# Expert outputs stored in tile order, fetched by slot in the attention that follows

## The reference

```python
# second experts: 4096 rows, two of 8 experts for each, at most 256 rows for each expert
top_vals, top_ids = top_k(x_flat @ router_w.T + router_b, 2)
top_probs = softmax(top_vals)
for e in range(8):
    tok, slot = nonzero(top_ids == e, size=256, fill_value=(N, 0))   # the first 256 rows
    y = (xin @ W[e]) * silu(xin @ V[e]) @ W_out[e]                   # xin = rows tok
    out[tok] += y * top_probs[tok, slot]
# third attention: keys and values from the normed context and from normed x (the latents),
# queries from the latents, 16 heads of 64
```

## Time and profile before

| | |
|---|---|
| time, median of three runs | 1677.85 us (1676.03 to 1679.96) |
| time of the profiled execution | 1677.99 us |
| its span, first to last instruction | 1676.1 us |
| TensorE matmul busy | 1402.1 us (84%) |
| VectorE busy | 1116.0 us (67%) |
| ScalarE busy | 894.4 us (53%) |
| GpSimd busy | 766.5 us (46%) |
| mean granted TensorE clock, share of full | 0.896 |
| queue of GpSimd's DMAs | 12448 packets, 26.21 MB |

### The profile page before, as it was taken

One profiled execution on the slowest core, in us unless ns is written; L12 is line 12 of the kernel. 1 busy time (PEld: TensorE's weight loads), 2 busy tenths in 40 slices (PEclk: granted clock), 3 DMA queues, 4 the chain that ended last, 5 costly groups with the idle time before them and its releaser, 6 DMA issues. The chain is left out here.

```text
span 1676.1 us, 37474 instructions
## 1 busy us (share of the span) xinstructions
PE 1402.1 (84%) x10866; PEld 1300.1 (78%) x10867; DVE 1116.0 (67%) x3509; ACT 894.4 (53%) x2715; POOL 766.5 (46%) x766
## 2 busy tenths in 40 slices
PE   6687699956867389999999999999998499567398
PEld 4566599945646289999999999999997499444298
DVE  5646744458777457777777777877776466686455
ACT  4454155532223168777878787778775133244254
POOL 3066345420003445555657575757454356303344
PEclk9797799977667789999999999999999699878599
DMA  9312112240131400000000000000000333521322
GB/s 223 41 33 60 49 56 63 63 157 24 51 110 41 127 13 2 14 1 19 9 15 11 1 24 0 25 0 13 1 14 9 105 82 85 191 66 52 114 78 71
DMA packets 88412, 88.54 MB, mean 53 GB/s; under 512 B 17058, under 2 KB 74761, under 8 KB 87927
## 3 DMA queue, kind: packets, MB, share of 16 engines
q1 hardware_dynamic: 72472, 58.10, 12.6%
q0 software_dynamic: 12448, 26.21, 4.8%
q10 hardware_dynamic: 3392, 3.02, 0.7%
HBM read 53.98 MB, written 34.82 MB: 53 GB/s over the span
## 5 line engine op out<-in xcount | busy, mean ns | idle before, releaser
L2101 POOL TENSOR_TENSOR paired_rows<-paired_rows,rinv 128x1024 f32<-128x1024 f32 x128 | 242.5, 1894 | 243.6 <-DVE rinv L2416 227.2
L2407 DVE TENSOR_TENSOR probs_turned_lo<-psum_banks,probs_turned_hi 128x512 fp32r<-128x512 f32 x256 | 175.9, 687 | 141.1 <-ACT probs_turned_hi L2266 137.5
L2292 ACT ACTIVATE paired_rows<-psum_banks,neg_max 128x256 f32<-128x256 f32 x512 | 236.7, 484 | 0.6 <-DVEq L1993 0.4
L2213 PE MATMUL psum_banks<-probs_turned_hi,y_rows 128*128 128x256 f32 x1024 | 213.9, 292 | 0.9 <-DVEq L1993 0.9
L2163 PE MATMUL psum_banks<-y_turned_parts,queries_hi 128*128 128x256 f32 x1024 | 199.7, 293 | 3.0 <-DVEq L1993 3.0
L2213 PEld LDWEIGHTS psum_banks<-probs_turned_hi,y_rows 128*128 128x128 f32 x1024 | 167.2, 190 | 1.7 <-DVEq L1993 1.5
L2266 ACT CAST probs_turned_hi<-psum_banks 128x512 fp32r<-128x512 f32 x256 | 151.2, 591 | 19.6 <-PE psum_banks L2134 9.6
L2163 PEld LDWEIGHTS psum_banks<-y_turned_parts,queries_hi 128*128 128x128 f32 x1024 | 158.1, 191 | 3.6 <-issue 3.6
L2134 PE MATMUL psum_banks<-ident,paired_rows 128*128 128x128 f32 x1024 | 155.6, 274 | 5.2 <-DVE probs_turned_lo L2407 2.9
L2422 DVE TENSOR_REDUCE neg_max<-psum_banks 128x4 f32<-128x1024 f32 x128 | 155.5, 1215 | 5.0 <-PE psum_banks L2163 4.7
L2163 PE MATMUL psum_banks<-y_turned_parts,queries_lo 128*128 128x256 f32 x512 | 144.8, 283 | 0.0
(11 more groups left out here) (718 smaller groups left out, 3734.0 us busy)
## 6 DMA issues: line engine op xcount, KB each, us to landing
paired_rows<-expert_rows SPq DMA_DIRECT2D x16, 512.0 KB, 6.0
expert_w_a<-rows_by_expert_last SPq DMA_DIRECT2D x39, 129.0 KB
tile_rows<-rows_by_expert_first SPq DMA_DIRECT2D x71, 64.5 KB
tile_rows<-rows_by_expert SPq DMA_DIRECT2D x71, 64.5 KB
expert_w_b<-in_L_ffn_w_dram SPq DMA_DIRECT2D x2, 2048.0 KB, 12.8
tile_rows<-expert_rows SPq DMA_DIRECT2D x8, 512.0 KB, 3.8
x_rows<-in_x_dram SPq DMA_DIRECT2D x8, 256.0 KB, 5.5
ctx_turned_dram<-ctx_turned SPq DMA_DIRECT2D x1, 2048.0 KB, 10.4
```

The lines of the kernel that those rows point to most:

```text
L2101: ins = pool.tensor_tensor(probs[:, k, :, :], probs[:, k, :, :], rinv[:, k, :].unsqueeze(2).to_broadcast([P, 4, 256]), ALU.mult)
L2213: ins = pe.matmul(bank[Z_BANK][:, r * 256:(r + 1) * 256], yrows[:, 2 * s1 + y, (2 * r + k) * P:(2 * r + k + 1) * P], probsT[x][:, (u + 1) ...
L2292: ins = act.activation(probs[:, par, h, :], bank[S_BANKS[par] + h // 2][:, (h % 2) * 256:(h % 2 + 1) * 256], ACT.Exp, bias=nmax[:, par, h: ...
L2407: ins = dve.tensor_tensor(lo, bank[bank_][:, :], hi.bitcast(F32), ALU.subtract)
```

## The change

The second experts no longer write to `ys` by pair. SyncE stores each output tile with a plain DMA of 64 KB at the tile's own place, so `ys` holds rows by slot; GpSimd only gathers. The routing keeps each pair's slot in `POS` (0 for dropped pairs, whose weight is zero) with four further columns of zeros, and no longer makes `DEST`: half of the one-hot matmuls and the VectorE operations behind them go. In the third attention a group's pairs are fetched by eight indirect gathers on GpSimd by these slots: two groups ahead of the loop, then each group in steps 13, 14 and 15 two cycles ahead of its use. Ahead of each eight, the slots of the group are copied to a small tile, GpSimd waits for that copy's semaphore, and does a tiny addition. Nine groups are fetched; the ninth, with the zero columns, is read by nobody.

```diff
-        POS = sb("slots", [P, 2, B], U32)
+        POS = sb("slots", [P, 2, B + G], U32)
@@ routing, VectorE
                     if capacity:
                         ch.link(dve.tensor_tensor(posf[:, :, :], posf[:, :, :], keep[:, :, :], ALU.mult))
+                        dve.memset(POS[:, :, B:B + G], 0)
+                        dve.tensor_copy(POS[:, :, 0:B], posf[:, :, :])
...
                     dve.tensor_scalar(SOURCE[:, 0:n_tiles], found, float(HALF), None, ALU.add)
-                    if layer in SCATTERED:
-                        ch.link(dve.tensor_copy(pair_used[:, :], first))
...
-                        dve.tensor_tensor(DEST[:, 0:n_tiles], pair_found[:, :], pair_spare[:, :], ALU.add)
@@ routing, TensorE, for each of eight pairs
-                            if layer in SCATTERED:
-                                k = r % top
-                                own = bank[7][:, (1 + k) * n_tiles:(2 + k) * n_tiles]
-                                ins = pe.matmul(own, hot_row[:, s, :, r], hot_tile[:, s, :, r], start=False, stop=True, skip_group_check=True)
@@ experts
-            expert_out = tile_scattered
+            scatters = not fixed
+            expert_out = tile_scattered if layer in KEPT else tile_loaded
@@ experts, SyncE
+                    if not scatters:
+                        for j in range(n_tiles):
+                            sp.wait_ge(expert_kept.sem, j + (expert_kept.value + 1))
+                            sp.dma_start(tile_of(ys, j), yo[:, j % SLOTS, :]).then_inc(expert_out[j % SLOTS].sem, 16)
+                        for s in range(SLOTS):
+                            sp.wait_ge(expert_out[s].sem, expert_out[s].value + 16 * in_slot(s))
@@ experts, GpSimd
-                        if i >= 0:
+                        if scatters and i >= 0:
@@ third attention, SyncE
-                    stage(0)
-                    stage(1)
                     load_expert_weights(sp, 2)
...
-                    stage(2)
-                    for n in range(3, NG):
-                        stage(n)
@@ third attention, GpSimd
+                    def gather_pairs(n, which):
+                        for x in which:
+                            j, k = x // 2, x % 2
+                            pool.indirect_dma_start(staged[:, j, k, :], None, ys[0:TILES_CAP * P, :], bass.IndirectOffsetOnAxis(ap=group_slots[:, x:x + 1], axis=0)).then_inc(pairs_staged.sem, 16)
+
+                    def slots_of(n):
+                        pool.tensor_copy(group_slots[:, :].rearrange("p (j k) -> p k j", k=2), POS[:, :, bass.ds(n * G, G)]).then_inc(slots_copied.sem, 1)
...
+                    GATHER = {13: (0, 1, 2), 14: (3, 4, 5), 15: (6, 7)}
...
+                    def begin_pairs(n):
+                        slots_of(n)
+                        pool.wait_ge(slots_copied.sem, n + 1)
+                        pool.tensor_tensor(slots_ready[:, 0:1], slots_ready[:, 1:2], slots_ready[:, 1:2], ALU.add)
@@ step
+                        if next_pairs_there(i) and c in GATHER:
+                            if c == 13:
+                                begin_pairs(i + 2)
+                            gather_pairs(i + 2, GATHER[c])
@@ ahead of the loop
+                    pool.memset(slots_ready[:, :], 0.0)
+                    begin_pairs(0)
+                    gather_pairs(0, range(2 * G))
                     norm_context(0)
+                    pool.wait_ge(pairs_combined.sem, 1)
+                    begin_pairs(1)
+                    gather_pairs(1, range(2 * G))
                     pool.wait_ge(turned_kept.sem, 1)
                     copy(0, 0, 0)
                     pool.wait_ge(turned_kept.sem, 2)
                     copy(0, 0, 1)
                     all_steps(step)(pool)
```

More of the change, by code:

```diff
@@ L278, in build @@
         leads_made = counter("leads_made")
+        slots_copied = counter("slots_copied")
         leads_exp = counter("leads_exp")
@@ L1331, in _ @@
                     dve.wait_ge(pe_done.sem, pv + 2 + (MADE if layer == 1 else 0))
-                    found, first, second = (bank[7][:, n * n_tiles:(n + 1) * n_tiles] for n in range(3))
+                    found = bank[7][:, 0:n_tiles]
                     dve.tensor_scalar(SOURCE[:, 0:n_tiles], found, float(HALF), None, ALU.add)
-                    if layer in SCATTERED:
-                        ch.link(dve.tensor_copy(pair_used[:, :], first))
[L1336 to L1343, removed]
-                        dve.tensor_tensor(DEST[:, 0:n_tiles], pair_found[:, :], pair_spare[:, :], ALU.add)
                 @block.scalar
@@ L1516, in _ @@
                                 continue
-                            to = xr[:, i % SLOTS, P:P + 1].bitcast(U32) if kept else DEST[:, i:i + 1]
+                            to = xr[:, i % SLOTS, P:P + 1].bitcast(U32)
                             pool.indirect_dma_start(ys, bass.IndirectOffsetOnAxis(ap=to, axis=0), yo[:, i % SLOTS, :], None).then_inc(expert_out[i % SLOTS].sem, 16)
-                    for s in range(SLOTS):
-                        pool.wait_ge(expert_out[s].sem, expert_out[s].value + 16 * in_slot(s))
+                    if scatters:
+                        for s in range(SLOTS):
+                            pool.wait_ge(expert_out[s].sem, expert_out[s].value + 16 * in_slot(s))
                 @block.tensor
@@ L1906, in attention_2 @@
                 group_scale = sb_in(ph, "group_scale", [P, 5, G])
+                group_slots = sb_in(ph, "group_slots", [P, 2 * G], U32)
+                slots_ready = sb_in(ph, "slots_ready", [P, 2])
                 weighted = carve(flat(Y1[:, :, :]), 16 * P, [P, G, P])
@@ L1935, in _ @@
                 def _(sp):
-                    pair_rows = ys[0:2 * B * P, :].rearrange("(t p k) d -> p t k d", p=P, k=2)
-                    def stage(n):
-                        if n:
-                            sp.wait_ge(pairs_combined.sem, n)
-                        sp.dma_start(staged[:, :, :, :], pair_rows[:, n * G:(n + 1) * G]).then_inc(pairs_staged.sem, 16)
-                    stage(0)
-                    stage(1)
                     load_expert_weights(sp, 2)
                     sp.dma_start(flat(Y1[:, 0:16, :]).rearrange("p (c d) -> p c d", d=P), A["L2_ffn_down_w"].rearrange("e (c p) d -> p (e c) d", p=P)).then_inc(weights_a.sem, 16)
-                    stage(2)
-                    for n in range(3, NG):
-                        stage(n)
                     place_pads(sp, range(E // 2))
@@ L1952, in _ @@
                     sp.wait_ge(rows_spread.sem, 16 * 2 * G * NG)
+                    sp.wait_ge(pairs_staged.sem, 16 * 2 * G * (NG + 1))
                     load_first_tiles(sp, 2)
@@ L2091, in spread, with next_pairs_there @@
                             pool.indirect_dma_start(xb, bass.IndirectOffsetOnAxis(ap=spots_of(n)[:, k, j:j + 1], axis=0), rows_of(n)[k][:, j, :], None).then_inc(rows_spread.sem, 16)
+                    GATHER = {13: (0, 1, 2), 14: (3, 4, 5), 15: (6, 7)}
+                    def next_pairs_there(i):
+                        return not isinstance(i, int) or 0 <= i < NG - 1
+                    def begin_pairs(n):
+                        slots_of(n)
+                        pool.wait_ge(slots_copied.sem, n + 1)
+                        pool.tensor_tensor(slots_ready[:, 0:1], slots_ready[:, 1:2], slots_ready[:, 1:2], ALU.add)
                     SPREAD = {3: (0, 1, 2), 6: (3, 4), 7: (5, 6), 8: (7,)}
@@ L2474, in _ @@
                     ch.link(dve.tensor_copy(ends, region))
-                    dve.wait_ge(pairs_staged.sem, 16)
+                    dve.wait_ge(pairs_staged.sem, 16 * 2 * G)
                     for k in range(2):
```

6 lines of the change are left out of this document (1 added, 5 removed).

## The result

The changed kernel takes 1684.49 us (median; 1677.71 to 1690.87) where the kernel before took 1677.68 in the same measurement (1672.88 to 1683.51). The ratio is 1.004, 95% interval 1.0027 to 1.0052, that is 6.7 us slower (4.5 to 8.7). The profiled execution took 1684.99 us, its span is 1683.1.

The account below looks back on a forecast made before the run. TensorE, 99% busy, was taken to bound the third attention's loop, but not the second experts or that attention's start. 1677.99 - 8.4 (routing and experts) + 17.1 (start) + 0 (loop) = 1686.7 us; own range 1682 to 1691, stated range 1678.0 to 1696.0.

Parts of the forecast that it names:

- Routing: End of the second routing: destinations and some TensorE waits go, a memset and copy come; 1.85 us earlier (1.4 to 2.3).
- the 0.45 for TensorE's waits: Routing: VectorE's three waits for TensorE shrink with halved matmuls; 0 to 0.9 us, taken as 0.45.
- Experts: Second experts: without scatters no tile waits for gathers; block ends 8.4 us earlier (7.0 to 8.9), routing's 1.85 included.
- the time of the last seven tiles: Second experts: after the eighth output, one more tile at 1.91 us and seven at 1.60 bring the last to 556.65.
- Start: Start of the third attention: GpSimd's gathers delay the first queries from 20.26 to 37.35 us after T0; 17.1 us lost.
- Pause: GpSimd's standstill at the third attention's start, read as a drain settling indirect DMAs; stays at 9.25 us, adding to gathers.
- Loop: Third attention's loop: 56 gathers fit beside TensorE; 0 us lost (0 to 0.5 a cycle, 3.5 in all).
- the pause was not hidden: Rival at the third attention's start: pause hidden or gone, drain costs 0.93 us, net +1.2, 1679.2 us; chance 0.20.
- did not come twice: Rival at the third attention's start: pause behind each eight gathers, 8.3 us more, 1695.0 us; chance 0.08.
- the loop's gathers kept to 1.032 us at most: Rival in the loop: stretched gathers at pitch 1.68, TensorE waits 14 us in all, 1700.7 us; chance 0.07.
- the experts did what they should: Rival in the second experts: the bound is something else, 4 us less gained, 1690.7 us; chance 0.03.
- The fourth: Rival at the third attention's start: pause shrinks, copies' drain free, queries within 25 us of T0, 1670.5 us; chance 0.07.

Follow-up runs that it names:

- the weights behind the pairs: Changed kernel plus a drain behind the experts' last gather, group 1 gathered behind the copies, weights' load issued after group 0's pairs landed: 1672.46 us, ratio 0.9959.
- plain loads: Changed kernel's routing and second experts with the third attention of the kernel before, no gathers there (adds other rows, same work): 1665.05 us, ratio 0.9901.
- the version between steps: Changed kernel plus drain behind the experts' last gather, group 1 gathered between the loop's first steps, weights after group 0's pairs: 1669.71 us; again 1669.62.

## Why the prediction was right, point by point

The forecast was +8.7 us against the profiled execution, the bold stages give +7.3 and the measurement +6.7. One sum of the prediction doesn't come out: the ends that it names for its own range (gain 7.0 to 8.9, loop up to 3.5, 2 us either way) give 1684.2 to 1693.6, and not 1682 to 1691. The result lies in both.

- **Routing**: 1.85 forecast, 1.7 found. The destinations' 1.66 went; the 0.45 for TensorE's waits was too much, as only one of the three gaps went.
- **Experts**: 6.55 forecast, 7.6 found. The step that was mis-sized is the time of the last seven tiles, which I took at 1.60 us each from a tile right behind a wait: 11.2 us. They took 10.0: one still 1.90, four 1.45, then 1.55 and 0.75. The store's landing was right (2.2 taken, 2.11 found, from the nearest rows of 2.1 and 3.8).
- **Start**: 17.1 forecast, 16.6 found. Preparation and eight gathers: 10.75 forecast, 10.5 found (564.97). Pause: kept whole at 9.25, found 8.92. Second eight gathers until 33.2, found 32.2 (586.64). The copies: their drain 1.55 us instead of 0.9. One more detail was wrong and cost nothing: the pairs landed at T0 + 13.96 and not by 12.5, with the weights' 3 MB, which SyncE now issues at 554.4 to 555.8, in flight beside them and the DMA engines 90% busy until then (the run with the weights behind the pairs has T0 + 12.07 and 18%); it stayed under the pause. As soon as the pause was short, GpSimd waited 1.03 us for VectorE.
- **The pause's cause**: right that it is the drain behind indirect DMAs and that 8 new ones neither hide nor double it. "Not linear in their number" holds as well. With all landed it is 2.77 us for 32, 7.26 for 87, 8.27 for 151 and 9.25 for 167: some 0.08 us for each between the first two, 0.02 and 0.06 between the others. For the 7.26 I had counted the 71 of the third experts; 16 scatters of the block before belong to it too, since no drain stands between. The 0.93 us after five isn't of this kind: the last of the five was issued from 1078.55 on and the drain ended at 1081.24, while the 16 gathers of the changed kernel's second experts land 2.5 us after their issue (median; 2.4 to 3.4). So I read a landing in it. These DMAs all move some 64 KB by 128 rows, so their number, rows and bytes aren't told apart, and what the drain does in that time no run here shows.
- **Loop**: 0 forecast, 0 found. The stage is 1.9 us longer than before in the profile, but as long with plain loads (709.18) and without the gathers (709.39). The 3.5 us that my range allowed for register waits rested on no row, and no run shows them: the cycles take 86.9 to 87.1 us with the gathers and without. The lateness is as worked out: steps 13 and 14 take 5.99 and 5.56 us (6.2 and 5.65 forecast), and step 15 catches up.
- **Rivals**: the pause was not hidden (8.92 against 0.93), did not come twice (1.55 behind the second eight), the loop's gathers kept to 1.032 us at most (beside what VectorE work, the last section says), and the experts did what they should. The fourth came near only by edits: queries at T0 + 24 in the version between steps, which it had put at "within 25 us".
- The step that I had named as the costly one, group 1's gathers ahead of the copies, holds: moving them away gave 6.4 us at the first queries. Less than their 9.85, since the latents (6.9 behind the context) then come last.

## What to carry to other kernels

Ask of an operation moved to another engine's queue what is queued behind it and who waits for that: 16 gathers at 1.27 us cost 16.6 us at the start of a block, where nothing else ran, and 56 cost nothing in a loop with idle GpSimd time in each step. A drain of GpSimd behind many indirect DMAs is a cost to be placed, not only paid: one early drain in an idle stretch is worth 5 us here. When an edit brings the first consumer forward, look at the second: 3 of the 6.4 us of the moved gathers came back as a late first scaling.

## What the runs showed of the hardware that I had not expected

- **GpSimd's drain took longer the more indirect DMAs lay between it and the last one**, with all of them landed: 2.77 us behind 32, 7.26 behind 87, 8.27 behind 151 (after GpSimd had stood idle for 15.65 us), 9.25 behind 167. Behind 8 that were still in flight it took 1.78 us, and 3.68 with 3 MB of weights in flight beside them; in both the next operation starts 0.44 us after VectorE, which waits for the landing, begins.
- **VectorE's combine stretches beside GpSimd.** Its eight operations (`x_rows<-tile_rows,mix_weights,x_rows`, two tensors in SBUF) take 2.35 us while GpSimd stands in its pause, and 3.18 to 3.85 us where GpSimd's context operations fall beside them, of which the second takes 1.15 or 1.16 instead of 1.04. In the kernel with the drain behind the experts' gathers two of the eight take 1.13 and 0.97 us where the others take 0.34, and each ends 0.15 us behind a GpSimd operation (571.69 behind 571.54, 572.99 behind 572.85). What holds them up there no run shows. The shorter pause of GpSimd came with 0.8 to 1.5 us more on VectorE.
- **The gathers were not stretched by a busy VectorE** in the loop: 942 to 1032 ns over all 72, beside 478 us of VectorE work in 628. But most of the VectorE work there takes a source from PSUM (`probs_turned_lo<-psum_banks,probs_turned_hi` and its like on L2418, and L2433: 63.4 of 69.5 us from 760 to 850), so how gathers fare beside copies within SBUF stays untested here.
